# Attention's projections on TensorE: three pairs instead of six single places in a step

## What is computed

```python
h = _layernorm(x) * (1 + ca) + sa
x = x + ga * _L0_attn_ref(h, Wq, Wk, Wv, Wo)
...
# _L0_attn_ref: 16 query heads, 4 key/value heads of 128, causal linear attention
q, k, v = x @ Wq.T, x @ Wk.T, x @ Wv.T        # as heads
q, k = rope(q), rope(k)
qf, kf = elu(q) + 1, elu(k) + 1
# at each position s:
state = state + k_s[:, None] * v_s[None, :];  z = z + k_s
num = q_s @ state;  den = q_s . z + 1e-6
out = (num / den) @ Wo.T
```

## Time and profile before

| | us |
|---|---|
| median of 3 runs | 1032.14 (1031.8 to 1033.04) |
| the profiled execution | 1031.37 |
| its span, first to last instruction | 1029.6 |
| TensorE busy | 976.8 (95%) |
| VectorE busy | 681.7 (66%) |
| ScalarE busy | 332.3 (32%) |
| GpSimd busy | 249.5 (24%) |

### The profile page before, as it was taken

How to read it: one execution, slowest core, us unless ns; L and a number is a source line. 1 busy time by engine, 2 the same in 40 slices (tenths; PEclk the granted TensorE clock), 3 DMA queues, 4 the chain that set the end, 5 groups by cost and what they waited for, 6 DMA issues and landing times. The chain is left out here.

```text
span 1029.6 us, 15693 instructions
## 1 busy us (share of the span) xinstructions
PE 976.8 (95%) x5994; PEld 791.1 (77%) x5994; DVE 681.7 (66%) x1494; ACT 332.3 (32%) x604; POOL 249.5 (24%) x320
## 2 busy tenths in 40 slices
PE   5899999999999999999978999998999999999997
PEld 4688888888888888888856788885666667778875
DVE  6766766666766667666565977765676776476556
ACT  4343333433333343334313323221122232422220
POOL 2232312222212323122201010023334554211011
PEclk9999999999999999999998999999999999999999
DMA  9400000000000000000004000002455340000000
GB/s 297 142 1 1 1 1 1 1 1 1 1 1 1 1 1 2 1 1 1 1 21 137 1 1 1 1 1 42 124 115 113 92 84 22 1 16 16 11 21 20
DMA packets 33051, 33.37 MB, mean 32 GB/s; under 512 B 6857, under 2 KB 26834, under 8 KB 32978
## 3 DMA queue, kind: packets, MB, share of 16 engines
q1 hardware_dynamic: 32978, 32.38, 11.9%
HBM read 23.98 MB, written 8.13 MB: 31 GB/s over the span
## 5 line engine op out<-in xcount | busy, mean ns | idle before, releaser
L396 POOL TENSOR_TENSOR rope_sum<-rope_cos,rope_sin 128x512 f32<-128x512 f32 x80 | 115.0, 1437 | 257.0 <-DVE rope_sin L517 257.0
L432 ACT ACTIVATE rope_exp<-rope_sum 128x512 f32<-128x512 f32 x80 | 50.5, 631 | 205.2 <-POOL rope_sum L396 205.1
L786 PE MATMUL proj<-wo_sb,attn_out_t 128*128 128x256 f32 x512 | 113.2, 379 | 0.7 <-issue 0.7
L786 PEld LDWEIGHTS proj<-wo_sb,attn_out_t 128*128 128x128 f32 x512 | 96.1, 190 | 13.4 <-issue 0.9
L735 PE MATMUL num<-v_ones,score_masked 128*128 128x129 f32 x512 | 99.2, 275 | 5.9 <-DVE score_masked L575 5.9
L736 PE MATMUL num<-state,q_t 128*128 128x129 f32 x512 | 99.0, 275 | 0.0
L2052 DVE SCALAR_TENSOR_TENSOR m_acc<-m_expert,gates,m_acc 128x256 f32<-128x256 f32 x128 | 61.9, 484 | 46.3 <-PE m_expert L2101 39.9
L735 PEld LDWEIGHTS num<-v_ones,score_masked 128*128 128x128 f32 x512 | 82.1, 191 | 13.4 <-DVE score_masked L575 8.0
L514 DVE TENSOR_TENSOR rope_cos<-proj,cos_sb 128x512 f32<-128x512 f32 x80 | 55.3, 691 | 52.3 <-PE proj L689 52.3
L689 PE MATMUL proj<-w_hi,a_h_hi 128*128 128x512 f32 x192 | 79.0, 493 | 4.1 <-DVE w_lo L139 2.4
L736 PEld LDWEIGHTS num<-state,q_t 128*128 128x128 f32 x512 | 77.7, 192 | 0.0
(11 more groups left out here) (250 smaller groups left out, 1883.6 us busy)
## 6 DMA issues: line engine op xcount, KB each, us to landing
kv_scratch<-t_kv SPq DMA_DIRECT2D x16, 256.0 KB, 2.4
kv_rows<-kv_scratch SPq DMA_DIRECT2D x32, 128.0 KB, 3.7
a_stage<-in_wqkv SPq DMA_DIRECT2D x6, 512.0 KB, 5.3
wo_sb<-in_wo SPq DMA_DIRECT2D x1, 2048.0 KB, 9.6
a_stage<-in_wgu SPq DMA_DIRECT2D x4, 512.0 KB, 9.7
out<-x_sb SPq DMA_DIRECT2D x16, 128.0 KB, 1.7
u_scratch<-u_rows SPq DMA_DIRECT2D x28, 64.0 KB, 2.9
t_u<-u_scratch SPq DMA_DIRECT2D x14, 128.0 KB, 2.2
```

The lines of the kernel that those rows point to most:

```text
L396: pool.tensor_tensor(y[:, parity], t1[:, parity], t2[:, parity], ALU.add).then_inc(s["y_done"], 1)
L786: mm = pe.matmul(proj[:, b, 0:D], o_t[:, i, :], wo[:, i, :], start=(i == 0), stop=(i == H - 1))
```

## The change

Only the order of TensorE's program in a step changes. p(1) moves from behind `q_turn(3)` to directly behind p(0); p(3) from behind `scores(3)` to directly behind p(2); p(5) from behind `out_turn(3)` to directly behind p(4). No instruction and no semaphore wait is added or removed, and the programs of the other engines stay as they are.

```diff
                     p(0)
+                    p(1)
                     numerators(0)
                     scores(1)
                     q_turn(3)
-                    p(1)
                     numerators(1)
                     out_turn(0)
                     scores(2)
                     p(2)
+                    p(3)
                     numerators(2)
                     out_turn(1)
                     scores(3)
-                    p(3)
                     numerators(3)
                     out_turn(2)
                     p(4)
+                    p(5)
 
                     pe.wait_ge(s["num_free"], at(c, b, KVH + 1, KVH + 1))
...
                     mm.then_inc(s["num_full"], 1)
                     out_turn(3)
-                    p(5)
                     if norm_on:
```

## The result

The changed kernel takes 1071.7 us (median of 4 runs) against 1031.97 of the kernel before: ratio 1.0358, 95% interval 1.033 to 1.0387. The prediction said 1071, range 1058 to 1077. One of the four executions took 1283.9 us at a mean clock of 0.748; the ratio leaves it out, and no trace shows what held it back. The profiled execution took 1071.15 us, 39.78 more than that of the kernel before.

What follows compares the result with a forecast made beforehand. TensorE, run in program order, bounds the attention stage; three uncovered waits, 0.77 + 1.06 + 0.76 = 2.59 us a step, give 39.1 us over 15 steps, so a median of 1071 us, range 1058 to 1077.

Steps and rivals of the forecast that it cites:

- TensorE's order is the bound, with 0.50 us of slack a step: Attention stage: TensorE in program order sets the 31.54 us step; its only idle time is 0.50 us before q_turn(1).
- Place 1: Before numerators(1), which p(1) leaves: 2.07 us chain through masked(1) against 1.30 us of work, a 0.77 us stall.
- Place 2: Between scores(3) and numerators(3), which p(3) leaves with no other work: 0.95 us plus 0.11 for the load, 1.06 us.
- The last step's bare wait: Last step, without projections: scores(3) ends at 528.04, numerators(3) starts at 528.99, showing an uncovered wait of 0.95 us.
- Place 3: Between out_turn(3) and the output projection, which p(5) leaves: wait for ScalarE's drain, 0.69 plus 0.07 for the load, 0.76 us.
- The three add: Each stall is measured from its own preceding TensorE group, so they sum to 2.59 us a step, 39.1 us in all.
- The pairs wait for nothing themselves: p(1) to p(5) and the state update, at their new times, find their inputs ready; none of them waits.
- entering a projection costs nothing that shows: The 491 against 396 ns of a projection's first two matmuls counted as 0 gain; as a price, 8.6 us saved.
- Rival B: Faster, about 1023 us: entering a projection costs 0.19 us and a pair pays it once, saving 8.6 us; 3%.
- rival D: The granted clock falls, about 1093 us or more: stalls bring half rate once a step, 22 us in all; 3%.
- The weight-load share: Loads fill 84% of a step; by the skill's rule some 5 us are free and the sum would be about 0.
- A sign that I had put wrong: In the profile after, TensorE idle before numerators(1), released by masked, about 0.6 to 0.8 us, 15 times.

Runs made afterwards that it cites:

- single moves: Three kernels, each the kernel before with only p(1), p(3) or p(5) moved next to its partner: ratios 1.0108, 1.0166 and 1.0135.
- both moves: Kernel before with next tile's k transposes and q_turn(0) moved beside the output projection, and VectorE's split of h moved earlier: 1026.98 us, ratio 0.992.
- when it was covered: Changed kernel, all three pairs kept, with out_turn(3) moved ahead of the state update's eight matmuls: 1061.25 us, ratio 1.0269 to the kernel before.
- the p(3) kernel: Kernel before with p(3) alone moved next to p(2), p(1) and p(5) left in place: ratio 1.0166.
- filling k's wait alone: Kernel before with next tile's k transposes ahead of the output projection and q_turn(0) inside it, VectorE's split unmoved: 1036.85 us, ratio 1.003.

## Why the prediction was right

- *TensorE's order is the bound, with 0.50 us of slack a step.* Held. The single moves lengthen the step by nearly their whole wait, and filling the 0.50 us (both moves) shortens it by 0.58.
- *Place 1, 0.77 us.* Measured 0.75 alone. In the changed kernel 0.66 from start to start, and the first pair of matmuls takes 0.32 (253.24 to 253.56) instead of 0.22. The same chain of VectorE: numerators(0) ends at 251.28, masked(1) starts at 252.50, 1.22 later, as in the earlier trace rows. The rows of the weight loads (PEld) fit the exposed load: in the running group a load begins 0.11 us ahead of its matmul (253.45 for the one at 253.56), the first, which needs the mask, only 0.01 ahead (253.23 for 253.24):

```profile
253.23 0.30 PEld L735 LDWEIGHTS num<-v_ones,score_masked 128*128 128x128 f32 x2 [0.73 <-DVE score_masked L575]
253.45 0.30 PEld L736 LDWEIGHTS num<-state,q_t 128*128 128x128 f32 x2
```

- *Place 2, 1.06 us.* Measured 1.03. The last step's bare wait was the right model: 262.51 - 262.30 to the mask, 263.25 - 262.30 = 0.95 to the matmul, there and here.
- *Place 3, 0.76 us.* Measured 0.73 alone and 0.76 when it was covered.
- *The three add.* Forecast 2.59 a step, measured 2.55, 2.51 as the sum of single moves. Forecast 39.1 us in all, measured 38.8 from first to last score; the other us lies outside the changed steps. That the time came within 0.7 us of the forecast is in part luck: the opening and the end alone moved by 1.8 and 0.8 us between the two profiled executions.
- *The pairs wait for nothing themselves, and entering a projection costs nothing that shows.* The second of a pair takes 249.50 - 248.09 = 1.41 us, like one that follows transposes. The mean of the first pass's rows fell from the 491 ns of the earlier trace rows to 442 mainly because only one projection a step, not two, is handed over while a score still streams: with p(3) alone moved it fell to 458, with p(1) or p(5) alone to 487 and 485. It was a mark of reading, not a price, as I had put it. Rival B's 0.19 us an entry is not there: each single move saves one entry, and came out only 0.02 to 0.03 us below its forecast wait.
- *The granted clock.* At 1.00 from 75 to 560 us in the changed kernel, so rival D did not come in the profiled execution. My argument against it was weaker than it read: that the last step kept a clock of 1.00 in spite of its waits holds of that execution, while with p(3) alone moved the same step had 0.83, as shown above. What speaks against D are the ordinary steps, 1.00 between 100 and 480 us in every trace. The changed kernel's stretch:

```profile
75.00:560.00 485.00, 452.11 (x2634) 372.92 (x2633) 289.47 (x565) 168.23 (x295) 109.20 (x96) 1.00 0.00 1
```

- *The weight-load share.* The rule of the Trainium skill (Perfetto Trace Analysis, Identifying the Most-Contended Engine) that this share shows the headroom would have left some 5 us a step free. The page gives the share, beside MFU (the rate of useful arithmetic), as a measure of the distance to the roofline; that busy time overstates, and that what the share leaves is free time in a step, was my reading of it. None of it was usable: a wait of 0.75 us cost 0.75 us, and where TensorE waited for nothing (both moves, above) the loads still filled no more than 322.75 / 380 = 85%. What did find the 0.58 us is the same page's Optimization Strategy: look for the gaps on the engine and at what releases them. The runs agree with that one.
- *A sign that I had put wrong.* I said that TensorE would be idle before numerators(1) for 0.6 to 0.8 us; that is so from start to start (0.66), but the row shows 0.49, with the tail of the transposes counted as busy. The cost is larger than the idle time in the row, by that tail and by the exposed weight load.

## What to carry to other kernels

In a step bound by one in-order engine, work that depends on nothing recent is worth most between a producer and the consumer that waits for another engine's answer: one piece for each such gap, and none twice in the same place. Price a gap by the chain (producer's end to consumer's start) minus the work left in it, and look in the kernel for a place where the same chain already runs bare; here the last step gave two of three terms. Compare kernels by the stretch that the change touches: the medians of the single moves carried 1.3 to 2.7 us from elsewhere. When a wait is filled, ask which input of the next instruction is now the latest: filling k's wait alone brought nothing until the split of h was early too.

## What the runs showed of the hardware

The granted clock in the opening, which the change does not touch, differs between executions. Of the first 40 us the profiled execution before had a mean of 0.96, the one after 0.90, and the first score came at 37.5 and 39.3 us. The last step, which is the same in the kernels of the single moves, took 16.1 us at a granted clock of 1.00 before and 19.0 us at 0.83 in the p(3) kernel. A few microseconds in a single execution are therefore no evidence on the change.

```profile
0.00:40.00 40.00, 24.62 (x101) 19.91 (x102) 27.12 (x44) 17.90 (x26) 11.15 (x19) 0.90 0.88 282
```

The window is the changed kernel's opening, its columns as in the earlier trace rows.
